# First attention: VectorE normalises eight heads at once, copies two banks of transposed probabilities at once, and joins two layer-norm waits

## What is computed

```python
kv = concatenate([memory, layer_input], axis=1)             # 128 keys for 64 queries
q, k, v = layer_input @ Wq, kv @ Wk, kv @ Wv                # 16 heads of 64
r = pe @ Wr
ac = einsum('bqhd,bkhd->bhqk', q + content_bias, k)
bd = rel_shift(einsum('bqhd,khd->bhqk', q + position_bias, r))
attn = softmax(where(mask, -1e9, (ac + bd) / sqrt(64)))
out = layer_norm(layer_input + (attn @ v) @ Wo)
```

## Time and profile before

| | us |
|---|---|
| median of 3 runs | 2005.97 |
| lowest and highest | 2002.24, 2006.39 |
| the profiled execution | 2001.38 |
| its span, from the first to the last instruction | 1999.8 |
| DVE busy in it | 1369.9 |
| PE busy in it | 1634.3 |

### The profile page before, as it was taken

How to read it: one execution, slowest core, us unless ns; L and a number is a source line. 1 busy time by engine, 2 the same in 40 slices (tenths; PEclk the granted TensorE clock), 3 DMA queues, 4 the chain that set the end, 5 groups by cost and what they waited for, 6 DMA issues and landing times. The chain is left out here.

```text
span 1999.8 us, 55013 instructions
## 1 busy us (share of the span) xinstructions
PE 1634.3 (82%) x17114; PEld 1295.9 (65%) x17114; DVE 1369.9 (69%) x4364; ACT 1171.9 (59%) x3299; POOL 942.3 (47%) x1373
## 2 busy tenths in 40 slices
PE   6999889898899677999999775449999885449882
PEld 6888778787787565777777562237777664337671
DVE  3778667676687556888777546868888774427673
ACT  2776657575666335777877432238888773127771
POOL 2354353334443345555666342444454444646773
PEclk8999999999999897999999796769999996559996
DMA  8766666565566003221000000000000000136765
GB/s 229 151 154 133 138 135 130 125 145 127 126 137 142 11 24 123 103 102 67 22 18 16 1 0 0 0 4 1 0 7 14 12 10 16 47 99 207 205 212 158
DMA packets 214845, 167.40 MB, mean 84 GB/s; under 512 B 27632, under 2 KB 188784, under 8 KB 214448
## 3 DMA queue, kind: packets, MB, share of 16 engines
q1 hardware_dynamic: 206128, 142.88, 28.6%
q0 software_dynamic: 8576, 22.88, 3.5%
HBM read 91.92 MB, written 73.76 MB: 83 GB/s over the span
## 5 line engine op out<-in xcount | busy, mean ns | idle before, releaser
L731 ACT ACTIVATE sb_probs<-sb_probs,sb_work 128x128 f32<-128x128 f32 x512 | 198.7, 406 | 168.0 <-DVE sb_work L636 168.0
L281 POOL TENSOR_SCALAR sb_next_var_eps<-sb_next_moments 128x1 f32<-128x1 f32 (+1 forms) x184 | 45.1, 245 | 468.0 <-DVE sb_next_moments L276 467.8
L883 POOL TENSOR_TENSOR sb_work<-sb_work,sb_cols 128x512 f32<-128x512 f32 x128 | 134.2, 1048 | 216.1 <-ACT sb_work L1100 134.5
L1026 DVE TENSOR_REDUCE sb_work<-PS 128x8 f32<-128x512 f32 x256 | 175.3, 685 | 46.2 <-PE PS L925 44.3
L1028 DVE TENSOR_TENSOR sb_work<-PS,sb_work 128x512 f32<-128x512 f32 x256 | 177.1, 692 | 8.8
L1060 ACT ACTIVATE sb_work<-sb_work 128x512 f32<-128x512 f32 x256 | 161.5, 631 | 32.9 <-DVE sb_work L1028 26.8
L899 PE MATMUL PS<-sb_ident,sb_work 128*128 128x128 f32 x1024 | 149.6, 286 | 15.4 <-ACT sb_work L1100 10.1
L952 PEld LDWEIGHTS PS<-sb_v_ones,sb_work 128*64 128x64 f32 x4096 | 132.2, 139 | 24.0 <-issue 15.5
L952 PE MATMUL PS<-sb_v_ones,sb_work 128*64 128x18 f32 x4096 | 144.1, 213 | 4.4 <-ACT sb_work L1066 3.0
L1066 ACT ACTIVATE sb_work<-PS 128x512 f32<-128x512 f32 x256 | 139.5, 595 | 9.3 <-PE PS L899 6.0
L899 PEld LDWEIGHTS PS<-sb_ident,sb_work 128*128 128x128 f32 x1024 | 113.4, 144 | 43.2 <-issue 31.2
(11 more groups left out here) (274 smaller groups left out, 4445.6 us busy)
## 6 DMA issues: line engine op xcount, KB each, us to landing
rel_scratch<-sb_work SPq DMA_DIRECT2D x64, 516.0 KB, 7.7
sb_work<-rel_scratch SPq DMA_DIRECT2D x64, 512.0 KB, 6.5
expert_rows<-sb_blank SPq DMA_DIRECT2D x36, 520.0 KB, 2.9
sb_w_up<-expert_halves SPq DMA_DIRECT2D x23, 512.0 KB, 3.8
sb_w_down<-expert_halves SPq DMA_DIRECT2D x23, 512.0 KB
expert_halves<-sb_e_halves POOLq DMA_DIRECT2D x16, 512.0 KB, 6.1
sb_work<-expert_rows SPq DMA_DIRECT2D x23, 260.0 KB, 3.3
sb_e_raw<-e_W POOLq DMA_DIRECT2D x16, 256.0 KB, 5.8
```

Source lines behind the costliest of these rows:

```text
L731: ins = e.activation(probs[:, j], probs[:, j], ACT.Exp, bias=neg_max[:, j:j + 1], scale=-1.0, accum_out=row_sum[:, j:j + 1])
L883: e.tensor_tensor(k_masked[:, u3], k_sb[:, u3].rearrange("p (b k) -> p b k", b=2).unsqueeze(2) .to_broadcast([P, 2, 4, S]), col("place").u ...
L1026: e.tensor_reduce(top, mine, AX.X, ALU.max).then_inc(sem("att_max_ready"), 1)
```

## The change

VectorE's `normalise` takes a half of the tile, eight heads, instead of a quarter: two calls with 8-wide reciprocals (L643 before) and products of 128x1024 (L645 before) replace four calls. The first half waits for the exponentials of groups 0 and 1 and stands where `normalise(0)` and `normalise(1)` stood; the second waits for all four groups and stands behind all four `keep_relative`, where `normalise(3)` stood. The copies into `probsT` become two of two banks each. TensorE waits for probabilities before groups 0 and 2 alone, and counts two copies in place of four. `add_relative` waits three times in place of four. The moments of `X` and of the context are computed in turns, statistics of both and then aggregates of both, behind one wait each. The arithmetic and the other engines' code stay.

```diff
@@ l0_tensor @@
-                        e.wait_ge(sem("l0_probs_ready"), 4 * n + g + 1)
+                        if g % 2 == 0:
+                            e.wait_ge(sem("l0_probs_ready"), 2 * n + g // 2 + 1)
...
-                        e.wait_ge(sem("l0_probsT_kept"), 4 * n + 1)
+                        e.wait_ge(sem("l0_probsT_kept"), 2 * n + 1)
...
-                        e.wait_ge(sem("l0_probsT_kept"), 4 * n + max(2 * G + 2, min(j + 2, 4)))
+                        e.wait_ge(sem("l0_probsT_kept"), 2 * n + (1 if j == 0 else 2))
@@ l0_vector @@
-                    wait_alone(e, sem("l0_scores_done"), 4 * t + g + 1)
+                    if g != 3:
+                        wait_alone(e, sem("l0_scores_done"), 4 * t + (1, 2, 4)[g])
...
-                def normalise(g):
-                    t, r = n + 1, slice(4 * g, 4 * g + 4)
-                    e.wait_ge(sem("l0_exp_done"), 4 * t + g + 1)
+                def normalise(half):
+                    t, r = n + 1, slice(8 * half, 8 * half + 8)
+                    e.wait_ge(sem("l0_exp_done"), 4 * t + 2 * half + 2)
                     e.reciprocal(row_inv[:, r], row_sum[:, r]).then_inc(sem("l0_inv_ready"), 1)
-                    e.wait_ge(sem("l0_inv_ready"), 4 * t + g + 1)
-                    e.tensor_tensor(probs[:, r], probs[:, r], row_inv[:, r].unsqueeze(2).to_broadcast([P, 4, KL]),
+                    e.wait_ge(sem("l0_inv_ready"), 2 * t + half + 1)
+                    e.tensor_tensor(probs[:, r], probs[:, r], row_inv[:, r].unsqueeze(2).to_broadcast([P, 8, KL]),
                                     ALU.mult).then_inc(sem("l0_probs_ready"), 1)
...
-                    for g in range(4):
-                        e.wait_ge(sem("l0_probsT_done"), 4 * n + g + 1)
-                        e.tensor_copy(probsT[:, 4 * g:4 * g + 4], PS[:, g].rearrange("p (i k) -> p i k", i=4))\
-                            .then_inc(sem("l0_probsT_kept"), 1)
+                    for half in range(2):
+                        e.wait_ge(sem("l0_probsT_done"), 4 * n + 2 * half + 2)
+                        e.tensor_copy(probsT[:, 8 * half:8 * half + 8].rearrange("p (g i) k -> p g (i k)", g=2),
+                                      PS[:, 2 * half:2 * half + 2]).then_inc(sem("l0_probsT_kept"), 1)
...
                     normalise(0)
-                    normalise(1)
...
                     keep_relative(1)
-                if has(1):
-                    normalise(2)
                 if has(3):
                     keep_relative(2)
                     keep_relative(3)
...
                 if has(1):
-                    normalise(3)
+                    normalise(1)
+                if has(0):
+                    wait_alone(e, sem("l0_out_added"), n + 1)
+                    if not has(3):
+                        x_moments_vector(e, "l0", n + 1, n, 1)
                 if has(3):
                     t = n + 3
                     wait_alone(e, sem("ctx_moments_kept"), t)
+                    if has(0):
+                        e.bn_stats(next_stats[:, 0], tile_of(n)).then_inc(sem("x_stats"), 1)
                     for b in range(2):
                         ins = e.bn_stats(c_stats[:, b], kv_in[0:S, (u + 3) % 4, b])
                     ins.then_inc(sem("ctx_stats"), 1)
                     wait_alone(e, sem("ctx_stats"), t + 1)
+                    if has(0):
+                        e.bn_aggr(next_moments[:, 0], next_stats[:, 0]).then_inc(sem("x_moments"), 1)
                     for b in range(2):
                         ins = e.bn_aggr(c_last[:, b], c_stats[:, b])
                     ins.then_inc(sem("ctx_moments"), 1)
-                if has(0):
-                    wait_alone(e, sem("l0_out_added"), n + 1)
-                    x_moments_vector(e, "l0", n + 1, n, 1)
```

More of the change, by code:

```diff
@@ L603, in l0_tensor, with tile_of @@
             ins.then_inc(sem("bases"), 1)
+        def tile_of(n):
+            return X[:, bass.ds(n, 1)].rearrange("p a d -> p (a d)")
         def l0_vector(e, c):
```

## The result

| | before | after |
|---|---|---|
| median us (runs) | 2005.78 (4) | 1957.01 (4) |
| lowest and highest | 2002.24, 2006.39 | 1954.30, 1959.49 |
| profiled execution, its span | 2001.38, 1999.8 | 1958.74, 1957.2 |

The ratio is 0.9763, with a 95% interval of 0.9748 to 0.9779: 44 to 51 us less, where 38 had been forecast. The mechanism that the prediction named did what it said, and a second gain of some 8.4 us, which it had put at zero, came with it.

A forecast was written before the change was run, and what follows sets the result against it. TensorE sets the first attention's tiles, but VectorE's waits for its own code stall the loop's turns. 1999.8 - 38.4 + 2.3 = 1963.7 us of span, plus 1.6 gives 1965.3, by the median 1969.9; stated 1968, range 1959 to 1976.

The forecast's parts named there:

- The mechanism that the prediction named: First attention's loop: VectorE refetches its code each turn; the changed body lies in three blocks, so five stalls go, -38.4 us.
- Turns, -38.4: First attention's loop turns: five turns at 7.7 us, PE's wait and the lower clock behind it, cost nothing any more.
- the rival above: From the experiments, on VectorE's instruction fetch: pages of 256 instructions, two kept, fit the five places too; no chance given.
- Normalising, copies, moments in the loop, 0: First attention's loop tiles: wider products and copies are covered by idle time, VectorE's savings gain nothing; 0 us.
- The cover for the copies: Loop tiles: two-bank copies of 1.23 to 1.38 us end before PE's L527 and first L535 want them; cost 0.
- The last steps, +2.3: From tile 28 on, uncovered: TensorE's last transposes wait for the wider product, L535 for a wider copy; +2.3 us, bounds 0 and +4.
- The stalls did not stay: Rival, first attention's turns: an engine keeps three blocks, five fetches remain, the rest is even; 2002 to 2006 us, chance 0.08.
- The gated layer's loop did not begin to stall: Rival: VectorE's later code moves by 101 instructions, this loop's one turn fetches too; 2009, up to 2013 us, chance 0.06.
- VectorE was not late for TensorE's ninth transpose in the loop: Rival: stalls go, but a held-up second product delays PE 0.9 us in half of 24 tiles; about 1979 us, chance 0.08.

The follow-up runs named there:

- moved kernels: Already met waits added ahead of VectorE's first-attention code: 64 on the kernel before, 1966.35 us; on the changed kernel 64, 1991.61 us, and 40, 1954.74 us (profiled execution).
- e1: Kernel before with 64 already met waits added at the head of VectorE's first-attention stream: 1966.35 us against 2001.49, ratio 0.9841.

## Why the prediction was right, and where it was not

**Turns, -38.4: right.** Five stalls went, and the tiles at a turn fell from between 25.3 and 26.5 to 17.87 to 17.92. What the text rested on, that blocks hold 128 instructions and that an engine keeps four, could not be read from the trace of before. Two moved kernels have confirmed what it said of the places. The window of two pages that the Trainium skill gives ("Runtime: NRT & Kernel Launch", section "Instruction fetch mechanics"), counted in the trace's 8 KB as the prediction counted it, would have kept the stalls, and did not. Counted in the Trainium skill's own pages, 16 KiB and 256 instructions, it is the rival above, which agrees with the places and not with the packets of 8 KB. Its 32 KiB are four blocks of the trace's 8 KB.

**Normalising, copies, moments in the loop, 0: this is the step that failed, a term put at nothing that measured 0.31 us a tile.** It says that "a gain on VectorE is worth nothing there" since PE was busy 17.95 of 18.00 us and its matmuls stood without gaps. But a busy PE does not say that PE had what it needed, and the 0.05 us that were missing lay just at the place: the seventh matmul of L535 starts 0.05 us after the end of the sixth and 0.64 after its start, where the others follow at 0.43. In the waits of before over the same 217 to 540 us as the earlier trace rows stood, next to the rows that I quoted:

```profile
PEld PS L535 <- DVE sb_x_lo L674: 12.3, 16, 0.9
```

The prediction says nothing of this line; weight loads overlap with matmuls, so it looks covered. The tile that starts at 332.57 in the trace of before shows that it was not: the subtraction, and the two weight loads that it releases.

```profile
338.91 0.42 DVE L674 TENSOR_TENSOR sb_x_lo<-PS,sb_x_hi 128x256 fp32r<-128x256 f32 x1
```

```profile
338.31 0.19 PEld L535 LDWEIGHTS PS<-sb_probsT,sb_kv_in 128*128 128x128 f32 x1 [0.24 <-issue]
339.38 0.30 PEld L535 LDWEIGHTS PS<-sb_probsT,sb_kv_in 128*128 128x128 f32 x2 [0.88 <-DVE sb_x_lo L674]
```

338.91 + 0.42 = 339.33, and the weights come at 339.38. In the changed kernel the same chain:

```profile
336.36 0.41 DVE L679 TENSOR_TENSOR sb_x_lo<-PS,sb_x_hi 128x256 fp32r<-128x256 f32 x1
```

```profile
336.82 0.19 PEld L536 LDWEIGHTS PS<-sb_probsT,sb_kv_in 128*128 128x128 f32 x1 [0.30 <-DVE sb_x_lo L679]
337.19 0.19 PEld L536 LDWEIGHTS PS<-sb_probsT,sb_kv_in 128*128 128x128 f32 x1 [0.19 <-issue]
```

The loads wait 0.30 and no longer 0.88, and they come one by one: the second is no longer pushed against the first. Some 27 tiles times 0.31 us (18.16 to 17.85) are 8.4, and 38.4 + 8.4 = 46.8 is what the start of the last queries moved, from 617.23 to 570.18 (47.05). With that term the sum for the profiled execution would have been 1956.9, where it was 1958.74. The cover for the copies was argued from L527 and the first L535, which do wait for them; the chain that starts with the copies and ends at the subtraction, three rows further on, was not followed to its reader.

**The last steps, +2.3: right in the wait, lucky in the sum.** TensorE's third group waits 2.02 us for the product in each of two tiles, as foreseen. But before, its waits there were 0.41 and 0.37 and another for ScalarE, ahead of the output product, of 0.6, which is gone, and the last L535 waits 0.5 less, where 0.3 more had been forecast. The sum at full clock is +1.0. The +2.5 of the profiled execution holds 1.4 of lower clock, which the prediction did not have.

**Rivals.** The stalls did not stay. The gated layer's loop did not begin to stall, the price of a state that the moved kernels exclude. VectorE was not late for TensorE's ninth transpose in the loop.

**From the sum to the runs.** In the profiled executions the first attention ends 44.6 us sooner (663.56 to 618.98), but the span is only 42.6 shorter. The rest, whose code is the same, took 1336.3 and 1338.2 us, and between 1334.3 and 1344.7 in the nine other traces that do the same work there. So up to 10 us between two executions come from the later phases. The medians differ by 48.8. The 4.6 us between median and profiled execution, a good half of them added to the forecast, are no larger than this spread. From 1965.3, the sum without them, the missing term leads to 1956.9, and from the stated 1968 to 1959.6; that the first is the median to the digit is luck.

## What to carry to other kernels

Before a loop is tuned, see whether its turn stalls: idle time for "issue" before the first instruction of an iteration, packets on the instruction queue in every iteration. Then it is the body's length and place in the stream that matter, and a body at the limit can gain 1.6% from instructions that do nothing in front of it (2001.49 to 1966.35 us here), or lose as much by an innocent edit. And a tile time is TensorE's own only if its weight loads wait for nobody: look at PEld's waits, follow each to the last instruction of its chain, and shorten that, once; parts that shorten the same chain do not add.

## What the runs showed of the hardware

- VectorE's code came in packets of 8 KB, one for some 128 instructions (marks at 58, 209 and 322 of a body, and at 41, 194 and 290 of another). A loop body that by this count touches three such blocks turned with 0.26 to 0.36 us of idle time (302 instructions 35 and 75 behind an edge, 338 at 11). One that touches four fetched five packets in each iteration and stood still for 6.9 to 7.2 us at each turn (338 at 75, 302 at 99).
- In all ten of these stalls the packet started 4.7 to 4.8 us after VectorE's last aggregate, and the first copy followed 2.1 to 2.4 us after that. The DMA engines were busy for 0.8 of that wait each time; no stall with quiet DMA engines is on record, so what part of it their load makes stays open.
- TensorE's weight load follows the end of the VectorE instruction that releases it by 0.05 us. A load that had to wait 0.88 us, in place of 0.30, put all later matmuls of the tile back by 0.31, with 0.05 us of idle time ahead of PE's matmul; at a turn of e1, where it waited 1.30, PE's idle time was 0.47.
- On VectorE, 128x1024 took 1.22 to 1.23 us both for the product in SBUF and for a copy out of two PSUM banks, against 0.69 for a single 128x512. Back to back the narrow ones overlap: four copies took 2.45 us and two wide ones 2.32, so merging a pair saved 0.07.
